# Moving all low halves of the hidden layer to VectorE, and the tokens' base and the last add to GpSimd

## The reference

```
x = x + relu(batchnorm(conv3x3(sign(layernorm over channels(x)), sign weights * alpha)))
t = tokens(x)                       # per image 3136 tokens of 128 channels
u = layernorm over channels(t)
w = u @ wr + br                     # one router weight per token
sel = the 1567 tokens of largest w
y = gelu(u[sel] @ w1 + b1) @ w2 + b2, times w[sel]      # hidden size 512
t = t + (u + y scattered to sel)
```

## Time and profile before

| | |
|---|---|
| median of three runs | 2616.55 us |
| span of the profiled execution, first to last instruction | 2610.8 us |
| its own time beside the span | not given apart; the median lies 5.75 us above the span |
| TensorE (PE) busy | 2300.4 us, 88% |
| VectorE (DVE) busy | 2136.8 us, 82% |
| ScalarE (ACT) busy | 1591.9 us, 61% |
| GpSimd (POOL) busy | 1585.5 us, 61% |

### The profile page before, as it was taken

How to read it: one execution, slowest core, us unless ns; L and a number is a source line. 1 busy time by engine, 2 the same in 40 slices (tenths; PEclk the granted TensorE clock), 3 DMA queues, 4 the chain that set the end, 5 groups by cost and what they waited for, 6 DMA issues and landing times. The chain is left out here.

```text
span 2610.8 us, 43327 instructions
## 1 busy us (share of the span) xinstructions
PE 2300.4 (88%) x10635; PEld 1629.5 (62%) x10635; DVE 2136.8 (82%) x5200; ACT 1591.9 (61%) x2926; POOL 1585.5 (61%) x1162
## 2 busy tenths in 40 slices
PE   7999999868888898989888888898888888888887
PEld 3555555456666666666666666666666666666665
DVE  6777777669989797989797878887989788889887
ACT  4444444356667566666666667666766666666664
POOL 1000000078788687778787778777878787868863
PEclk9999999979999898999898989998999998989998
DMA  4434444411111111111111111111111121212101
GB/s 156 162 148 174 159 150 177 153 42 57 67 67 67 67 66 67 66 67 66 67 66 67 66 67 66 67 66 67 66 67 69 64 76 57 77 56 77 67 30 54
DMA packets 60455, 217.75 MB, mean 83 GB/s; under 512 B 22224, under 2 KB 27056, under 8 KB 56368
## 3 DMA queue, kind: packets, MB, share of 16 engines
q1 hardware_dynamic: 60192, 216.31, 23.0%
q10 hardware_dynamic: 144, 0.30, 0.0%
HBM read 136.70 MB, written 77.47 MB: 82 GB/s over the span
## 5 line engine op out<-in xcount | busy, mean ns | idle before, releaser
L315 POOL TENSOR_TENSOR hl<-hs,hh 128x448 fp32r<-128x448 f32 x672 | 863.4, 1308 | 7.7 <-ACT hh L510 7.7
L508 ACT ACTIVATE hs<-ps,b1c 128x448 f32<-128x448 f32 x896 | 573.2, 640 | 171.2 <-PE ps L944 165.0
L510 ACT ACTIVATE hh<-ps,b1c 128x448 fp32r<-128x448 f32 x896 | 577.3, 644 | 0.0
L429 POOL TENSOR_TENSOR tl<-tr,th 128x448 fp32r<-128x448 f32 x224 | 279.3, 1247 | 360.7 <-ACT th L532 353.1
L858 PE MATMUL ps<-yo,cwT 128*128 128x448 bf16 x2016 | 425.3, 356 | 0.0
L942 PE MATMUL ps<-th,w_h 128*128 128x448 f32 x896 | 395.5, 441 | 0.0
L954 PE MATMUL ps<-hh,w_h 128*128 128x448 f32 x896 | 380.7, 425 | 0.0
L944 PE MATMUL ps<-th,w_l 128*128 128x448 f32 x896 | 349.9, 390 | 0.0
L943 PE MATMUL ps<-tl,w_h 128*128 128x448 f32 x896 | 349.6, 390 | 0.0
L955 PE MATMUL ps<-hl,w_h 128*128 128x448 f32 x896 | 333.2, 372 | 0.0
L956 PE MATMUL ps<-hh,w_l 128*128 128x448 f32 x896 | 331.4, 370 | 0.0
(11 more groups left out here) (127 smaller groups left out, 4622.7 us busy)
## 6 DMA issues: line engine op xcount, KB each, us to landing
xb<-x SPq DMA_DIRECT2D x31, 1568.0 KB, 7.5
xb<-x SPq DMA_DIRECT2D x33, 896.0 KB, 4.7
result<-yo SPq DMA_DIRECT2D x32, 896.0 KB, 4.5
y_int<-y SPq DMA_DIRECT2D x32, 784.0 KB, 3.8
xb<-x SPq DMA_DIRECT2D x33, 672.0 KB, 4.4
result<-yo SPq DMA_DIRECT2D x32, 672.0 KB, 3.1
y<-y_int SPq DMA_DIRECT2D x32, 448.0 KB, 5.2
y<-y_int SPq DMA_DIRECT2D x32, 336.0 KB, 5.6
```

Source lines behind the costliest of these rows:

```text
L315: ops.tensor_tensor(hl[(b + c) % 2][:, j, :], hs[:, j, :], hh[(b + c) % 2][:, j, :].bitcast(f32), ALU.subtract).then_inc(hl_pool if on_poo ...
L429: nc.gpsimd.tensor_tensor(cut(tl, c), tr[(b + c) % 2][:, :], cut(th, c).bitcast(f32), ALU.subtract).then_inc(tl_ready, 1)
L508: nc.scalar.activation(hs[:, j, :], ps[:, H_BANK + j, 0:T], ACT.Gelu_apprx_tanh, bias=b1c[:, j:j + 1])
L510: nc.scalar.activation(hh[(b + slot) % 2][:, j, :], ps[:, H_BANK + j, 0:T], ACT.Gelu_apprx_tanh, bias=b1c[:, j:j + 1]).then_inc(hh_ready, 1)
```

## The change

Every low half of the GELU's output goes to VectorE, at the same positions as before, with a single semaphore `hl_ready`. `token_base` and `add_base` go from VectorE's program to GpSimd's, at the same positions, behind the residual and the low part of that position. The base on GpSimd gets a wait on `out_ready` of the image two back (the buffer's last reader), and `centre_tokens` gets one on `base_ready` (the ring buffer `tr` has now a reader on another engine).

```diff
-POOL_LOW_BLOCKS = ((0, 1, 2, 3), (1,), (2,), (0, 1, 2, 3), (0, 1, 3), (0, 1, 2, 3), (0, 1, 2, 3))
-POOL_LOW = [(c, j) for c, blocks in enumerate(POOL_LOW_BLOCKS) for j in blocks]
...
         def wait_low(eng, n, c, j):
 
-            on_pool = (c, j) in POOL_LOW
-            rank, total = low_blocks[on_pool].index((c, j)), len(low_blocks[on_pool])
-            eng.wait_ge(hl_pool if on_pool else hl_dve, n * total + rank + 1)
-
-        def low_hidden(eng, ops, n, b, pos, on_pool):
+            eng.wait_ge(hl_ready, (n * NCH + c) * NB + j + 1)
+
+        def low_hidden(n, b, pos):
 
             c, j = divmod(pos - LOW_LAG, 2 * NB)
-            if j < NB and c >= 0 and ((c, j) in POOL_LOW) == on_pool and has(n):
-                eng.wait_ge(hh_ready, (n * NCH + c) * NB + j + 1)
-                ops.tensor_tensor(hl[(b + c) % 2][:, j, :], hs[:, j, :], hh[(b + c) % 2][:, j, :].bitcast(f32),
-                                  ALU.subtract).then_inc(hl_pool if on_pool else hl_dve, 1)
+            if j < NB and c >= 0 and has(n):
+                nc.vector.wait_ge(hh_ready, (n * NCH + c) * NB + j + 1)
+                nc.vector.tensor_tensor(hl[(b + c) % 2][:, j, :], hs[:, j, :], hh[(b + c) % 2][:, j, :].bitcast(f32),
+                                        ALU.subtract).then_inc(hl_ready, 1)
...
+            def add_base(m, b, c):
+                g = m * NCH + c
+                pool.wait_ge(gated, g + 1)
+                pool.wait_ge(base_ready, g + 1)
+                nc.gpsimd.tensor_tensor(cut(yo[b], c), cut(yo[b], c), cut(base[b], c),
+                                        ALU.add).then_inc(out_ready, 1)
+
+            def token_base(m, b, c):
+                g = m * NCH + c
+                pool.wait_ge(t_ready, g + 1)
+                if has(m - 2):
+                    pool.wait_ge(out_ready, (m - 2) * NCH + c + 1)
+                nc.gpsimd.tensor_tensor(cut(base[b], c), cut(xb[b], c), tr[(b + c) % 2][:, :],
+                                        ALU.add).then_inc(base_ready, 1)
+
             def phase2(n, b):
                 for pos in range(POS):
-                    low_hidden(pool, nc.gpsimd, n, b, pos, True)
...
                         low_part(m, mb, c)
+                    for m, mb, c in due([p + 1 for p in OUT_AT], -1, n, b, pos):
+                        add_base(m, mb, c)
+                    for m, mb, c in due(BASE_AT, 1, n, b, pos):
+                        token_base(m, mb, c)
...
                 wait_count(dve, tl_ready, g - 1)
+                wait_count(dve, base_ready, g - 1)
                 V.tensor_tensor(tr[ring][:, :], ur[ring][:, :], ps[:, BC1, 0:T], ALU.subtract).then_inc(t_ready, 1)
```

More of the change, by code:

```diff
@@ L247, in block_kernel @@
         hh_ready = sem("hh_ready")
-        hl_dve = sem("hl_dve")
-        hl_pool = sem("hl_pool")
+        hl_ready = sem("hl_ready")
         y_done = sem("y_done")
@@ L299, in done @@
             return (n + shift) * len(steps) + (sum(p < pos for p in steps) - sum(p - POS >= pos for p in steps))
-        low_blocks = {True: sorted(POOL_LOW),
-                      False: sorted({(c, j) for c in range(NCH) for j in range(NB)} - set(POOL_LOW))}
         def wait_low(eng, n, c, j):
-            on_pool = (c, j) in POOL_LOW
-            rank, total = low_blocks[on_pool].index((c, j)), len(low_blocks[on_pool])
-            eng.wait_ge(hl_pool if on_pool else hl_dve, n * total + rank + 1)
-        def low_hidden(eng, ops, n, b, pos, on_pool):
+            eng.wait_ge(hl_ready, (n * NCH + c) * NB + j + 1)
+        def low_hidden(n, b, pos):
             c, j = divmod(pos - LOW_LAG, 2 * NB)
-            if j < NB and c >= 0 and ((c, j) in POOL_LOW) == on_pool and has(n):
-                eng.wait_ge(hh_ready, (n * NCH + c) * NB + j + 1)
-                ops.tensor_tensor(hl[(b + c) % 2][:, j, :], hs[:, j, :], hh[(b + c) % 2][:, j, :].bitcast(f32),
-                                  ALU.subtract).then_inc(hl_pool if on_pool else hl_dve, 1)
+            if j < NB and c >= 0 and has(n):
+                nc.vector.wait_ge(hh_ready, (n * NCH + c) * NB + j + 1)
+                nc.vector.tensor_tensor(hl[(b + c) % 2][:, j, :], hs[:, j, :], hh[(b + c) % 2][:, j, :].bitcast(f32),
+                                        ALU.subtract).then_inc(hl_ready, 1)
         MASK_STEPS = 7
@@ L776, in apply_gate @@
                 V.tensor_tensor(cut(yo[b], c), cut(yo[b], c), ps[:, BC1, 0:T], ALU.mult).then_inc(gated, 1)
[L778 to L782, removed]
             def phase2(n, b):
@@ L796, in phase2 @@
                         gates(m)
-                    low_hidden(dve, V, n, b, pos, False)
+                    low_hidden(n, b, pos)
                     for m, mb, c in due(TRANSPOSE_AT, 1, *at):
@@ L817, in phase2 @@
                         split_stats(m)
[L818 to L821, removed]
                     for m, mb, r in rounds:
```

## The result

| | before | changed |
|---|---|---|
| median, us | 2616.32 (2615.28 to 2624.36, 4 runs) | 2745.31 (2743.3 to 2747.49, 4 runs) |
| ratio to before | 1 | 1.049, 95% interval 1.0468 to 1.0512 |
| profiled span, us | 2610.8 | 2741.2 |

The change makes the kernel 4.9% slower. The direction was forecast (chance 0.66), but 2667 us was not the time, and 2745 lies 17 us above the range's upper end of 2728.

The account below looks back on a forecast made before the run. TensorE and VectorE were taken to be late by turns. S 0.6, T 0.8 and M 0.2 make 1.6 us a turn, times 31 turns 49.6, plus 0.5 at the end: +50, 2667 us; 8-in-10 range 2597 to 2728.

Parts of the forecast that it names:

- S: Position 34 over the turn's end to 2, VectorE sets the time: work +1.6, waits -1.0, so +0.6 us a turn.
- my upper bound of +0.3: Waits in S if tiny instructions wait as now and 11 low halves 0.22 us each: 9.0 us, +0.3.
- rival (a): Waits inside VectorE's instructions in S grow +0.8 us; S +2.4, turn +3.4, 2722 us; chance 0.15 together with (d).
- a third of GpSimd's instructions in S is gone: Argument against growing waits in S: GpSimd has 14 instructions there where it had 21, load down by factor 0.62.
- rival (b): Waits in S fall with GpSimd's load, -3.1 us; S -1.5, turn -0.7, 2595 us; chance 0.2.
- T: Positions 3 to 11: four more low halves delay TensorE's transposes 1.6 us, hidden every second turn; mean +0.8 us.
- M: Positions 12 to 33, TensorE sets the time: VectorE's extra work costs nothing, GpSimd's late low part +0.2 us.
- my bounds of 0 and 1.1: In M, delay of the router's matmul by GpSimd's low part behind its power: 0 to 1.1 us, 0.2 taken.
- +0.5 us against 3.3 us idle: In M, VectorE's six low halves more, three adds and two bases less, fit its idle time: cost nothing.
- the tiny L740: Sign: a tiny search-chain instruction on VectorE in S would have a mean under 0.679 but well over 0.3 us.
- some tens: Sign: the router's wait for GpSimd's low part, nearly nothing before, would show some tens of us at the most.
- (d): Low halves come late for ScalarE as VectorE's lag passes four positions: +62 us on top; chance 0.15 with (a).

Follow-up runs that it names:

- e12: Changed kernel with the seven bases back on VectorE (all low halves on VectorE, last adds on GpSimd): 2617.07 us, ratio 1.0000 to before.
- e11: Changed kernel with the seven last adds back on VectorE (all low halves on VectorE, bases on GpSimd): 2735.95 us, ratio 1.0452 to before.
- e3: Kernel before with all 28 low halves on VectorE; bases and last adds stay on VectorE too: 2662.81 us, ratio 1.0161 to before.
- e8: Changed kernel with GpSimd's 14 bases and adds cut from 448 columns to one, most of their work left out: 2439.93 us, ratio 0.9312 to before.
- hinted kernels: Kernel before and changed kernel, each with a prefetch hint for the closing branch of VectorE's second-phase loop: 2543.19 us and 2739.68 us.
- e5: Kernel before with a prefetch hint for the closing branch of VectorE's second-phase loop: 2543.19 us, ratio 0.9701 to before.
- e7: Changed kernel with GpSimd's base of position 17 and add of position 20 put behind the router's last low part: 2715.57 us, ratio 1.036 to before.
- e14: Kernel before with the prefetch hint and the search chain's two tiny instructions rewritten as tensor_scalar: 2446.90 us, ratio 0.9328 to before.
- e17: Changed kernel with the prefetch hint on VectorE's second-phase loop: 2739.68 us, ratio 1.0453 to before.
- e6: Kernel before with 24 long-met waits added to VectorE's loop body: 2617.63 us, ratio 0.9995 to before.
- e9: Kernel before with 48 long-met waits added to VectorE's loop body: 2619.33 us, ratio 1.0007 to before.
- e16: Kernel before with VectorE's loop head moved to the start of a fetch block: 2618.57 us, ratio 0.9997 to before.
- e13: Changed kernel with the search chain's two tiny instructions rewritten as tensor_scalar with one SBUF tensor input: 2641.81 us, ratio 1.0075 to before.

## Why the prediction was wrong

**Direction: right, for part of the reasons.** VectorE's work grows and its waits do not fall.

**S, forecast +0.6, measured +2.1.** The work, +1.6 by count, fits. The waits inside VectorE's two-input instructions in S were taken to fall from 8.7 to 7.7 us. Over the same 24 turns, and with the prediction's least times, they are 8.6 before and 9.0 after (14 tiny instructions 5.5, 12 low halves 3.5): +0.4 for a forecast -1.0. That is about my upper bound of +0.3 and short of rival (a)'s +0.8. The step that failed is "a third of GpSimd's instructions in S is gone", as a ground for fewer waits: the mean tiny instruction waits 0.39 us for 0.47, but 26 instructions are there to be hit, and a low half waits 0.29 for the assumed 0.22. Nor is a third gone: by the table's cut GpSimd is busy for 17.0 us of S with 13 instructions, for 22.2 with 17 before, a factor of 0.77 and not 0.62. The tiny instructions' waits over the kernels:

| | before | changed | e12 | e11 | e3 |
|---|---|---|---|---|---|
| GpSimd busy in S, us | 22.2 | 17.0 | 13.1 | 11.9 | 7.3 |
| 14 tiny instructions wait, us a turn | 6.6 | 5.5 | 2.7 | 3.2 | 1.2 |

So the waits go down with GpSimd's load in the rough, as rival (b) had it, but the 14 instructions that GpSimd was given bring most of them back. The reason that I gave for little change, that a gate's end releases GpSimd's add into VectorE's next instruction, fits the changed kernel, but no run moves these adds to other places of S. e8 shows the size of what was at stake: the additions that GpSimd was given are worth 305 us with all that follows.

**T, forecast +1.6 and 0, measured +1.8 and -3.9.** The turn without the pause came as forecast, and between hinted kernels T gives +1.8 in the mean of both turns (11.1 to 12.9). In the opening turn I took VectorE's 1.96 us of idle time for slack; it was one more effect of the pause at the loop's head (with the hint, in e5, all of VectorE's waits at that line are 5.6 us for 59.5), and the pause stands in the trace as a wait for nothing that the profile shows:

```profile
1510.33 0.89 DVE L649 BATCH_NORM_STATS2 st<-ps 112x6 f32<-112x128 f32 x4 [3.12 <-issue]
```

I had not read this row, though it is 34.4 us of the groups. The pause's cost of 74 to 78 us nearly all went away with the change, and masked a third of the loss.

**M, forecast +0.2, measured +2.9: the term that failed most.** By positions it is +0.5 (12 to 26), +1.0 (27 to 32) and +1.4 (33). The +1.0 is TensorE's wait for GpSimd's low part, which I had costed: it is inside my bounds of 0 and 1.1, but I took 0.2. In the turn shown the four instructions behind the power take 1.4 us apiece for my 1.25, and the last low part 1.5 for 1.2. e7 takes 1.4 of the 2.9 us back by order alone. The other 1.9 us I had put at nothing, and that is the step that failed: "+0.5 us against 3.3 us idle", costed as nothing. VectorE's idle time in M lies at L710 and at the gates, where it waits in its order, and not where its work was added; it is still idle for 4.4 us of M in the changed kernel. e3 loses 2.6 us in M with no base or add on GpSimd, most of it ahead of position 27. I had also not asked who waits for the router's result, VectorE at L710 with the low halves behind it, but e7 gives this only 0.3 us of position 33.

**The signs.** VectorE's busy time per turn is 60.6 us for a forecast 58, the low half's mean 872 ns for 750 to 850, the tiny L740 502 ns, inside its bounds. The transposes' wait for L685 grew, from 53.8 to 66.0 us. TensorE's wait for the counts is shorter (62.0), which was to speak for rival (b), yet (b) is wrong: the waits moved behind the gates. The wait of the router for GpSimd's low part, 65.5 us in 89 places, is above the "some tens". (d) did not come: 15.7 us.

**The sum.** Between hinted kernels the change costs 1.0453 less 0.9701, 197 us: the low halves 108, the bases and adds on GpSimd the other 89; by stretches S +1.3, T +1.8 and M +3.0 us a turn. Of the 197, 68 are given back because the pause's cost goes from 78 to 10 us. That leaves 129. So the time came nearer to the forecast by luck: I did not know of the pause that hid a third of the loss, and between hinted kernels the forecast of +50 is 147 us short and not 79. One slip is in the prediction's arithmetic: S between 0 and +1.3 gives 2648 to 2688 us by its own sum, not 2635 to 2700.

**A faster version.** e14, the kernel before with the hint and the one-input search instructions, takes 2446.9 us, 169 less than before and 298 less than changed.

## What to carry to other kernels

Before moving a two-input instruction between VectorE and GpSimd, ask which instructions it will run beside: here rewriting two tiny instructions of a chain to one SBUF input and a per-partition scalar was worth 45 to 103 us, for 46 that the whole move of the low halves cost. Idle time of an engine is room for more work only where it lies: time that it stands in its order at one instruction does not help work that is queued behind it. Read the rows that wait for "issue" at a loop's head before calling any idle time in that pass slack, and try the hint early.

## What the runs showed of the hardware

**The loop branch.** VectorE issues nothing for 3.46 us behind each of the 12 taken branches of the kernel before; ScalarE, TensorE and GpSimd go on after some 0.2 us or less. With the hint VectorE takes 0.3 us in e5 and 0.5 in e17. The Trainium skill (Runtime: NRT & Kernel Launch, Instruction fetch mechanics) states that a taken branch whose target lies outside the fetched window stalls until the target is fetched. The pauses and the hint's effect agree with it; where the window lies no run shows, as e6, e9 and e16 did not move the pause. Why it is 2.8 us in most kernels with all low halves on VectorE, but 3.4 in e13, which has the changed kernel's 528 records, is open.

**A releaser can be named wrongly.** In the changed kernel the same pause is put down to TensorE, whose transposes ended at 1297.49, 0.6 us before:

```profile
1295.44 0.62 DVE L704 TENSOR_TENSOR tr<-ur,ps 128x448 f32<-128x448 f32 x1
1298.10 0.89 DVE L658 BATCH_NORM_STATS2 st<-ps 112x6 f32<-112x128 f32 x4 [2.04 <-PE ps L882]
```

**A `tensor_scalar` may be held as well.** In e14 an instruction that takes 241 ns in the kernel before, in e5 and in e13 has

```profile
L751 DVE TENSOR_SCALAR mk<-wk,srch 98x32 f32<-98x32 f32 x29 | 26.6, 916 | 2.3
```

though it has one large SBUF operand; I read this as a wait for GpSimd's instruction. The search instructions, of one column, are not held (270 and 214 ns). Which of them enters a two-port mode is not shown here.
